# Mixture of experts behind attention: routed experts in 128-row tiles of the tokens that chose them, all behind the last round

## The reference

```python
scores = softmax((x @ wt.T + g @ wg.T per sequence) / 2)     # 8 experts
topk_w, topk_idx = top_k(scores, 2); topk_w = topk_w / topk_w.sum(-1)
gp = leaky(einsum('th,ehm->etm', x, w_gate))                  # 8 experts of width 128
up = einsum('th,ehm->etm', x, w_up)
y_all = einsum('etm,emh->eth', gp * up, w_down)
y = sum over the two chosen e of y_all[e, t] * topk_w
p = leaky(x @ sw_gate) * (x @ sw_up) @ sw_down                # shared, width 256
x = x + y + p
```

## Time and profile before

| | us |
|---|---|
| median of 3 runs | 1171.68 (1171.07 to 1172.27) |
| profiled execution: span from first to last instruction | 1168.5 |
| profiled execution: its own time outside the span | not recorded apart from the runs above |
| TensorE, VectorE, ScalarE, GpSimd busy | 1083.2, 776.2, 526.6, 443.5 |
| moved by DMA | 89.75 MB |

### The profile page before, as it was taken

How to read it: one execution, slowest core, us unless ns; L and a number is a source line. 1 busy time by engine, 2 the same in 40 slices (tenths; PEclk the granted TensorE clock), 3 DMA queues, 4 the chain that set the end, 5 groups by cost and what they waited for, 6 DMA issues and landing times.

```text
span 1168.5 us, 21036 instructions
## 1 busy us (share of the span) xinstructions
PE 1083.2 (93%) x6572; PEld 867.9 (74%) x6572; DVE 776.2 (66%) x2536; ACT 526.6 (45%) x1565; POOL 443.5 (38%) x422
## 2 busy tenths in 40 slices
PE   2478899999999999999999999999999999999888
PEld 1366697778777787777877787777877779777777
DVE  7679668764776658675587647766486756866443
ACT  3059625552455515654255524555146542555111
POOL 3155333442534414543334415344145433353212
PEclk9589999999999999999999999999999999999989
DMA  5146302311121211321123111222113211221033
GB/s 198 43 148 203 113 23 88 98 47 55 56 92 64 64 56 56 100 64 40 54 91 96 50 55 56 92 64 64 56 55 100 64 37 44 91 93 50 33 99 119
DMA packets 40819, 89.75 MB, mean 77 GB/s; under 512 B 4008, under 2 KB 18864, under 8 KB 40192
## 3 DMA queue, kind: packets, MB, share of 16 engines
q1 hardware_dynamic: 40704, 88.28, 23.5%
HBM read 78.66 MB, written 11.70 MB: 77 GB/s over the span
## 4 chain that ended last, share of the span: by engine, by line
PE 77%; DVE 12%; issue 6%; POOL 2%; ACT 1%; SPq 1%; DMA 0%; DVEq 0%; POOLq 0%; ACTq 0%
PE psY L1458 12%; PE psG L60 7%; PE psS L60 6%; PE psG L62 6%; PE psG L61 6%; PE psS L62 6%; PE psO L1391 6%; PE psS L61 6%; PE psT L1372 4%; PE psS L1357 2%; PE psO L1394 2%; PE psT L1379 2%; PE psT L60 2%; PE psT L62 2%; PE psT L61 2%
## 5 line engine op out<-in xcount | busy, mean ns | idle before, releaser
L548 POOL TENSOR_TENSOR work<-work,rden 128x514 f32<-128x514 f32 x128 | 134.2, 1049 | 362.9 <-DVE rden L1023 362.9
L675 ACT ACTIVATE work<-work,low 128x257 f32<-128x257 f32 x256 | 127.9, 502 | 90.5 <-DVE low L1042 89.8
L1458 PE MATMUL psY<-Wd,H 128*128 128x256 f32 x640 | 156.0, 387 | 0.0
L60 PE MATMUL psS<-KB_hi,qT_hi 128*128 128x512 f32 (+1 forms) x256 | 121.2, 473 | 18.7 <-DVE low L1042 12.6
L1134 DVE SCALAR_TENSOR_TENSOR leaky<-leaky 128x512 f32<-128x512 f32 x80 | 60.2, 752 | 110.7 <-ACT leaky L707 109.7
L1458 PEld LDWEIGHTS psY<-Wd,H 128*128 128x128 f32 x640 | 116.4, 190 | 22.3 <-issue 8.4
L60 PE MATMUL psG<-x1T_hi,Wgu 128*128 128x512 f32 x280 | 124.9, 446 | 0.1
L1042 DVE CUSTOM_DVE_ANT_0 work<-psS,bias,null_s 128x256 f32<-128x256 f32 x256 | 112.8, 477 | 13.7 <-PE psS L1357 12.8
L535 POOL TENSOR_TENSOR rq<-qss,neghalf 128x16 f32<-128x16 f32 x32 | 93.7, 2930 | 52.2 <-DVE qss L1017 52.2
L62 PE MATMUL psG<-x1T_lo,Wgu 128*128 128x512 f32 x280 | 110.8, 396 | 0.0
L61 PE MATMUL psG<-x1T_hi,Wgu 128*128 128x512 f32 x280 | 109.8, 392 | 0.0
(11 more groups left out here) (246 smaller groups left out, 2732.7 us busy)
## 6 DMA issues: line engine op xcount, KB each, us to landing
Wgu<-wexp SPq DMA_DIRECT2D x80, 512.0 KB, 3.3
Wb<-wscr SPq DMA_DIRECT2D x64, 256.0 KB, 3.5
wexp<-Wgu SPq DMA_DIRECT2D x10, 512.0 KB, 2.9
xin<-in_x SPq DMA_DIRECT2D x8, 512.0 KB, 4.1
xres<-in_x SPq DMA_DIRECT2D x8, 512.0 KB, 4.0
out<-work SPq DMA_DIRECT2D x8, 512.0 KB, 3.0
H<-in_wgu SPq DMA_DIRECT2D x10, 256.0 KB, 3.5
bscr<-bscr SPq DMA_DIRECT2D x1, 2048.0 KB, 12.5
```

The lines of the kernel that those rows point to most:

```text
L60: te.matmul(dst, a_hi, b_hi, start=start, stop=False)
L548: pool.tensor_tensor(T1[sl][:, hs, :], T1[sl][:, hs, :], rden[sl][:, 1, hs].unsqueeze(2) .to_broadcast([P, 2, N + 1]), ALU.mult)
L675: act.activation(T1[sl][:, h, :], T1[sl][:, h, :], ACT.Exp, scale=-1.0, bias=low[sl][:, 1, h:h + 1], accum_out=den[sl][:, 1, h:h + 1])
L1458: mm = te.matmul(psY[:, t // 2, (t % 2) * D:(t % 2 + 1) * D], H[:, k % H_RING, t * P:(t + 1) * P], Wd[:, ORDER[k], :], start=(k == 0 and t ...
```

## The change

The rounds keep attention, the router and the two shared experts. Their result (x1 plus shared part) goes to DRAM as `base`. The routed experts leave the rounds. In each round TensorE counts by small matmuls (`ranks`) how many tokens before each one chose the same expert, VectorE makes row numbers from it (`positions`), and GpSimd writes each token's x1 row with its weight as 257th number to `xg` in DRAM twice, to the place of its first and of its second expert, by 8 indirect DMAs (`scatter`). Two rounds are a segment. At its end `tile_table` makes a table of 23 tiles (`SEG_TILES`): the first row and the expert of each. There are always 23, enough for any choice, 92 in all (`UNITS`). `STARTS` and `GATHER_FROM` are empty, so `UNIT_AT` is too, `IN_LOOP` is 0, and all tiles stand behind round 7. A tile is turned, multiplied with its expert's gate and up in plain f32, weighted, turned, multiplied with down, and stored to `yg`. Last, GpSimd gathers for each of 32 chunks of 128 tokens the two rows of `yg` and adds them to `base` in SBUF by accumulating indirect DMAs (`gather`); 24 chunks are put between the tiles by `CHUNK_AT`, 8 follow them. The hardware loop over the rounds is written out.

In the diff below, the loops over `u` at its end are, in this order, those of SP, ScalarE, VectorE and TensorE.

```diff
-ORDER = list(range(E, BLOCKS)) + list(range(E))
-H_RING = 3
-W_RING = 3
+SEG_ROUNDS = 2
+SEGS = ROUNDS // SEG_ROUNDS
+SEG_TILES = 2 * SEG // P + E - 1
+UNITS = SEGS * SEG_TILES
+X_RING, G_RING, D_RING, C_RING = 3, 3, 4, 3
-GATE_AT = {1: 3, 3: 4, 5: 5, 7: 6, 10: 7, 12: 8, 14: 9}
+STARTS = {}
+UNIT_AT = {}
+IN_LOOP = len(UNIT_AT)
+RANK_AT, SCATTER_AT, WEIGHT_AT, SCATTER2_AT, TABLE_AT = 1, 3, 6, 7, 4
...
+        x_banks = [psG[:], psY[:, 0, :], psS[:, 0, :], psS[:, 1, :]]
+        y_banks = [psY[:, 1, :], psO[:], psT[:, 0, :], psT[:, 1, :]]
...
+            def load_tile(u):
+
+                last = (u // SEG_TILES + 1) * SEG_ROUNDS - 1
+                if u % SEG_TILES == 0:
+                    need(sp, table_done, u // SEG_TILES, 1)
+                    stand(sp, waited_sp)
+                    for e in range(E):
+                        end = sp.value_load(fill[0:1, u // SEG_TILES, e:e + 1], min_val=0,
+                                            max_val=(SEGS - 1) * ROWS + E * ROOM - P)
+                        sp.dma_start(xg.ap()[bass.ds(end, P), :], zeros.ap()).then_inc(fill_in.sem, 16)
+                    need(sp, fill_in, u // SEG_TILES, 16 * E)
+                    stand(sp, waited_sp)
+                    need(sp, scatter_a, last, 16 * TILES)
+                    stand(sp, waited_sp)
+                    need(sp, scatter_b, last, 16 * TILES)
+                    stand(sp, waited_sp)
+                row, expert = row_of(u), expert_of(u)
+                need(sp, ge_done, 0, u - X_RING + 1)
+                stand(sp, waited_sp)
+                sp.dma_start(xe[:, u % X_RING, :], xg.ap()[bass.ds(row, P), :]).then_inc(xe_in[u % X_RING].sem, 16)
+                need(sp, gu_ps, 0, u - G_RING + 1)
+                stand(sp, waited_sp)
+                sp.dma_start(We[:, u % G_RING], wgu[bass.ds(expert, 1)].rearrange("a p w c m -> p (a w) c m")) \
+                    .then_inc(we_in[u % G_RING].sem, 16)
+
+            def load_down(u):
+                expert = expert_of(u)
+                need(sp, ye_ps, 0, u - D_RING + 1)
+                stand(sp, waited_sp)
+                sp.dma_start(Wde[:, u % D_RING, :], wdown[:, bass.ds(expert, 1), :].rearrange("p a d -> p (a d)")) \
+                    .then_inc(wde_in[u % D_RING].sem, 16)
...
+            for u in range(IN_LOOP, UNITS + 5):
+                if u < UNITS:
+                    load_tile(u)
+                    load_down(u)
+                if IN_LOOP <= u - 5:
+                    store_tile(u - 5)
+                if u in CHUNK_AT:
+                    load_base(CHUNK_AT[u])
+                    if CHUNK_AT[u] - 2 in CHUNK_AT.values():
+                        store(CHUNK_AT[u] - 2)
+            for c in range((SEGS - 1) * SEG_CHUNKS, ROUNDS * TILES + 2):
+                if c < ROUNDS * TILES:
+                    load_base(c)
+                store(c - 2)
...
+            for u in range(IN_LOOP, UNITS + 4):
+                if IN_LOOP <= u - 1 < UNITS:
+                    weigh_gate(u - 1)
+                if u < UNITS:
+                    copy_tile(u)
+                if IN_LOOP <= u - 3 < UNITS:
+                    copy_hidden(u - 3)
...
+            for u in range(IN_LOOP, UNITS + 5):
+                if IN_LOOP <= u - 1 < UNITS:
+                    leak_tile(u - 1)
+                if IN_LOOP <= u - 4 < UNITS:
+                    take_tile(u - 4)
+                if IN_LOOP <= u - 1 < UNITS:
+                    hide_tile(u - 1)
...
+            for u in range(IN_LOOP, UNITS + 4):
+                if IN_LOOP <= u - 4 < UNITS:
+                    expert_down(u - 4)
+                if u < UNITS:
+                    expert_turn(u)
+                if IN_LOOP <= u - 1 < UNITS:
+                    expert_gate_up(u - 1)
+                if IN_LOOP <= u - 2 < UNITS:
+                    expert_turn_hidden(u - 2)
```

More of the change, by code:

```diff
@@ new lines, in gather @@
+            def gather(c, slot):
+                m, t, b = c // TILES, c % TILES, c % C_RING
+                if slot == 0:
+                    if c % (SEG_ROUNDS * TILES) == 0:
+                        total = (m // SEG_ROUNDS + 1) * SEG_TILES
+                        for i in range(2):
+                            need(pool, ye_out[i], 0, 16 * len(range(i, total, 2)))
+                    need(pool, cb_in[b], 0, 16 * (c // C_RING + 1))
+                else:
+                    need(pool, gather_a[b], 0, 16 * (c // C_RING + 1))
+                pool.indirect_dma_start(out=cb[:, b, :], out_offset=None, in_=yg[m // SEG_ROUNDS].ap(),
+                                        in_offset=bass.IndirectOffsetOnAxis(
+                                            ap=back[:, m // SEG_ROUNDS, m % SEG_ROUNDS, slot, t:t + 1], axis=0),
+                                        compute_op=ALU.add) \
+                    .then_inc((gather_a, gather_b)[slot][b].sem, 16)
@@ L574, in _ @@
+            for c in range(done, ROUNDS * TILES + 1):
+                if c < ROUNDS * TILES:
+                    gather(c, 0)
+                if c - 1 >= done:
+                    gather(c - 1, 1)
         @block.scalar
@@ L636, in attention @@
                         turned_q(r, u)
-                    if n == 1 and moe is not None:
-                        weights(moe)
+                    if (r, n - 3) in UNIT_AT:
+                        copy_hidden(UNIT_AT[r, n - 3])
                     if n >= VALUE_LAG:
@@ L973, in attention @@
                 if moe is not None:
-                    for t in range(TILES):
-                        sums(moe, t)
                     need(dve, ysum, moe, TILES)
+                    need(dve, scatter_b, moe, 16 * TILES)
                 ch, cx = vchain["ln2"], vchain["x1"]
@@ new lines, in expert_turn_hidden, with expert_down @@
+            def expert_turn_hidden(u):
+                need(te, he_done, 0, u + 1)
+                need(te, ye_done, 0, former(u, y_no) + 1)
+                te.transpose(y_banks[y_no(u)][:, 0:P], he[:, u % 2, :], ident[:]).then_inc(he_ps.sem, 1)
+            def expert_down(u):
+                need(te, wde_in[u % D_RING], 0, 16 * (u // D_RING + 1))
+                need(te, heT_done, 0, u + 1)
+                te.matmul(y_banks[y_no(u)][:, D:2 * D], heT[:, u % 2, :], Wde[:, u % D_RING, :], start=True,
+                          stop=True).then_inc(ye_ps.sem, 1)
@@ L1422, in gate_up @@
             def gate_up(m, k, w, bank):
                 for c in range(KC):
-                    mm = products(te, bank, [Wgu[:, k % W_RING, part, w, c, :] for part in range(2)],
+                    mm = products(te, bank, [Wgu[:, k, part, w, c, :] for part in range(2)],
                                   [part[:, c, :] for part in x1T], c == 0, c == KC - 1)
@@ L1472, in _ @@
             attention(0, None, 1)
-            with te.Fori(1, ROUNDS - 1) as r:
-                attention(r, r - 1, r + 1)
-            attention(ROUNDS - 1, ROUNDS - 2, None)
+            for r in range(1, ROUNDS):
+                attention(r, r - 1, r + 1 if r + 1 < ROUNDS else None)
             m = ROUNDS - 1
```

663 lines of the change are left out of this document (427 added, 236 removed).

## The result

| | median us | lowest to highest | ratio to before, 95% interval |
|---|---|---|---|
| before | 1171.38 | 1169.79 to 1172.27 | |
| after | 1519.57 | 1516.03 to 1522.78 | 1.2977, 1.2953 to 1.3 |

The change makes the kernel slower by 348 us. The forecast was 1500 (1350 to 1670). Medians and ranges are over four or more executions of each version, and no version fell into a slow state. The profiled execution has a span of 1517.6 us.

The account below looks back on a forecast made before the run. It took TensorE to bound the old rounds, and a circle through SP, TensorE and ScalarE at half clock the tiles. First tile 956 + tiles 442 + chunks 18 + switches 33 + drain 8 + end 45 + 3 gave 1505, rounded 1500 (1350 to 1670).

Parts of the forecast that it names:

- surcharge for the half clock: In the tiles, TensorE at 1.2 GHz lengthens a step from 4.05 to 4.8 us; half clock with the circle had chance 0.45.
- What the rounds give back: Rounds without routed experts: 108 us each instead of 135.9, gain 195 us, last projection moving from 1106.5 to 911.
- the wait for the writes: In each round, VectorE's second weight column waits for GpSimd's first four row writes to land; 0.7 us net.
- Up to the first tile: From the last projection at 911: 16.4 + 13 + 16 us, so first transpose at 956.
- The tiles: 92 tiles behind the rounds at 4.8 us a step, 442 us; TensorE's own part 1.55, SP alone 3.7.
- the ScalarE circle: In the tiles, down, turn, gate/up and ScalarE's weigh and copies close on themselves: 2.7 us, or 4.1 at half clock.
- the circle of SP and TensorE: In the tiles, from a down through SP's queue to landed rows 5.4 us, then 2.7, over two steps: 4.05 us a step.
- Rival (b): In the tiles, register loads or SP issues are dearer, 1.3 us a load, SP alone 5.7 a tile: 1610 us; chance 0.15.
- Switches, end: Three more segment switches with register loads and zero-row fills, 33 us; last segment's 8 chunks behind the tiles, 45 us.
- (a): Rival: full clock in the tiles, 92 steps of 4.05 us, 1435 us in all; chance 0.25.
- (c): Rival: landing is faster and SP runs ahead, only ScalarE's circle binds, 2.8 us a tile: 1305 us; chance 0.10.
- (d): Rival: tiles overlap, TensorE alone sets a step at 1.55 us, rounds give their full 36 us: 1100 us; chance 0.04.

Follow-up runs that it names:

- warm: Against after, twelve small bf16 matmuls per tile added on TensorE ahead of its wait for the tile's rows; 1516.0 us.
- late2: Against after, the second weight column and second four row writes stand at steps 9 and 10 of the rounds, not 6 and 7; 1499.8 us.
- allbehind: Against after, all 32 chunks of gathers follow the last tile, none between the tiles; 1607.0 us.
- static_d6: Against after, fixed tile addresses without SP register loads, six down-weight buffers instead of four, routed part of the result left out; 1410.1 us.
- combo: Against after, six down-weight buffers, one register load less per tile, later second row writes, zero rows written in rounds 3, 5 and 7; 1397.6 us.

## Why the prediction was right

The direction held, and so did the kind of mechanism: four dependent pieces for one tile close circles through SP and ScalarE, and a step costs three times the 1.55 us of TensorE's work. That the number came within 20 us is in part luck. The surcharge for the half clock isn't borne out by warm, and three terms that the forecast had too small (the loops of the rounds, SP's list, the chunks) made up for it. By its steps:

- **What the rounds give back.** 111.1 us a round against 108, and the last projection ends at 935.5, not 911. Of these 24.5 us, 2.7 are round 0, which is within the spread above. The part ahead of the loop is right: 40.8 to 41.1 for 40.9. The loop is the term that was mis-sized: 70.2 in the mean of rounds 1 to 7, for 66.4 and 0.7. First, the wait for the writes is 2.1 us a round, not 0.7 net; a write takes 0.96 us on GpSimd with some 0.3 behind it, and late2 gives 1.6 a round back. Second, the tile table, which the prediction set against the weight splits that go. It stands in rounds 2, 4 and 6, and their loops are 3.8 to 5.5 us longer than those of rounds 1, 3 and 5 (2.0 us a round in the mean of seven). In the chain that ended last it stands whole, from 314.40 to 318.6 in round 2, behind the scores and ahead of the division on GpSimd, and nothing hides it; no run took it out or moved it:

```profile
314.13 0.27 DVE work L1251
314.40 0.15 DVE tcmp L1351
...
318.38 0.19 DVE back L1375
318.58 0.19 DVE rden L1224
...
318.84 1.04 POOL work L688
```

- **Up to the first tile.** 935.5 to 981.1 is 45.6, forecast 45.
- **The tiles.** The 91 steps from the first turn (981.1) to the last (1457.0) take 475.9 us; less 37 for the switches they are 4.82 each, forecast 4.8 and 18 for the chunks, 5.0. The sum came out nearly right by errors that cancel. Landing takes 2.1 us, not 3.0. SP alone needs 3.92 (four issues, three loads), not 3.7, and with the ring of four the step is 4.33 in the first segment. (The prediction's 645 KB a tile are 640.5 by the sizes on the page of after: 128.5, 256, 128 and 128; nothing hangs on it.) Chunks add 35 to 44 us (by allbehind, and by 66 steps of 4.99 less 4.33), not 18, since SP also waits in its one queue for gathers to land.
- **The clock.** This is the step that no run bears out. The prediction let the half clock lengthen a circle of 4.05 to 4.8, 69 us in 92 tiles. The granted clock did fall (0.50 to 0.76 over stretches of 50 us, changing between the two levels from step to step), but warm raised it and gained 3.6 us of 1519, within its own spread. The rest is open, since the added matmuls took back a part of what the clock gave. Full and half clock do set the ScalarE circle, 2.75 and 4.31 in static_d6. At the measured landing the circle of SP and TensorE would be (4.5 + 2.7)/2 = 3.6 at the full clock, under SP's own 3.92, and (4.5 + 4.1)/2 = 4.3 at the half clock, above it: so the clock may have a part in the 0.4 us by which the first segment's step (4.33) is over 3.92, where the forecast charged 0.75.
- **Register loads.** Two lie between the store and the next rows, 1.72 us in combo's queue, 1.36 beyond the issue itself, with 1.4 forecast. One load less makes SP's list 3.34 instead of 3.92: 0.58 us. The Trainium skill, DMA: Bandwidth & Descriptors, "Latency and other measured facts", gives a floor of about 600 ns for such a load; the trace agrees. Rival (b), 1.3 us, falls.
- **Switches, end.** 12.3 us extra for each switch against 11; from the last product to the end 52 us against 45, two chunks taking 10.7 and not 10.
- **Rivals.** (a), full clock, 1435: warm has most of that clock and 1516, though with the added matmuls. (c), SP ahead, is what static_d6 shows in its first segment, 2.83 a step. (d), overlap, needs a step of 2.3 us or less; the shortest mean of a segment in any version with the tiles behind the rounds is 2.83.

## What to carry to other kernels

Before work is cut into small pieces with computed addresses, add up what one piece costs on the queue that issues it: four issues and three register loads were 3.9 us here against 1.55 of matmul. That was the first bound, not the only one: without the loads and with the longer ring a tile still took 2.8 us in the first segment and 3.9 to 4.0 beside the chunks. Follow a tile around all engines and divide by the number in flight; in-order engines that serve all tiles make "four in flight" worth less than it says. A low clock on an engine that waits may be a sign of the wait rather than its cause; only a run that raises the clock without adding work would tell. Small operations that are put into a full loop, like the tile table, are not hidden because they are small: look whether the engine's next result is waited for.

## What the runs showed of the hardware

- An indirect write of 128 rows of 257 f32 holds GpSimd for 0.96 us, an accumulating indirect gather of 128 rows of 256 f32 for 1.54 us; a gather lands 4.4 us after its issue.
- Granted clock in the tiles goes between 1.00 and 0.50 from one step to the next (four gate/up matmuls take 1.91 us at 1102.70, where it is 0.52 over their time, and 1.03 at 1106.75, where it is 1.00). Twelve small bf16 matmuls a tile lift the mean from 0.55 to 0.84 in 1095 to 1165. The Trainium skill, TensorE: Matmul & The Clock Gate, "Part 4: PE-mode transpose", has transposes not counting as activity; after neither held one level nor the other, so the run doesn't decide it.
